# Audio tower on one core: raw loads issued by GpSimd, transfers in 48, 80 and 12 rows, stacks in runs of 8832 bytes

## The chip, the cores and the metric

The kernel runs on one core of one Trainium2 chip. The metric is the device time of one execution in microseconds (us). Of three runs the median is 657.14 us (654.91 to 658.24). The engines are called PE (TensorE matmul), PEld (its weight load), DVE (VectorE), ACT (ScalarE), Pool (GpSimd) and SP (SyncE, which here only issues transfers).

## What is computed

x is (128, 90, 750) in float32: 128 clips, 90 channels. Of each clip 46 patches of 16 samples are embedded into 192 numbers; causal attention without heads follows, and then a block of 12 heads whose q, k and v have a routed low-rank addition:

```python
patches = x[:, :, :46*16].reshape(B, 90, 46, 16).transpose(0, 2, 1, 3).reshape(B, 46, 1440)
h = einsum('bnf,ef->bne', patches, W_tok) + b_tok
n = layernorm(h); s = (n @ Wq) @ (n @ Wk).T, masked below the diagonal
h = h + softmax(s) @ (n @ Wv)
n = layernorm(h)
probs = softmax(n @ W_gate.T + b_gate)            # 8 experts, the best 2 are used
qkv = n @ W_qkv.T + b_qkv + sum_e top2(probs)_e * 2 * (n @ A_e.T) @ B_e.T
out = h + attention_12_heads(qkv) @ W_proj.T + b_proj
```

## The kernel before

**Tiling.** The clips go through in 16 groups of 8 (368 tokens: three token tiles, or four pairs of two clips with 92 rows). Each matmul operand is split into a high and a low float16 part, and a product is three or five matmuls (`split_product`, `deep_product`, lines 1314 to 1325). For the raw clips ACT copies the high part (`high`, line 735 via `high_of_x`) and Pool subtracts the low part (`low`, line 641): 8 and 16 instructions for each group, the first half for clips 0 to 3, the second for clips 4 to 7. The last 4 samples of each patch go to a tile `xe` first, and SP moves them to spare rows of `xs` (`extra_rows`, line 501).

**Schedule.** Five engine programs each run 24 steps. An operation `op` works in step s on group s - LAG[op]; the order within a step is written out by hand at the end of each engine's `step`. All waits are semaphores, and each engine and each transfer queue works in program order. PE's step holds `xt(0)` (transposes of the normalised h, lag 3) ahead of `tok(0)`, the first products with `xs` (lag 2). Before it come `sc`, the qk products, `av`; behind it the attention of heads.

**Pool's step.** Splits `low(5)` to `low(7)` of group s-1, `ad` (lag 4, waits for DVE's `disp`), `low(8)`, `low(9)`, `ln1(0)`, `low(10)` to `low(15)`, `ln1(1)`, `h2b`, `ln1(2)`, `ln2`, `xn2`, then `low(0)` to `low(4)` of group s. `ln1(t)` works on group s-2 and gives scale and offset (`rs`, `nb`) of token tile t; ACT's `xn_tile(t)` (line 910) uses them, and PE's `xt(0)` (line 1404) needs all three tiles. DVE's `h2_` (line 1187) needs Pool's `h2b` (line 699) of two groups before, and frees the bank that `xt(0)` writes.

**SP's queue.** All transfers are issued by SP, in one queue: in the prologue the patch weights, the two halves of group 0, the early weights, the first extra rows; then in each step

```python
                qk_to_scratch()
                load_next(1)
                stack_qk()
                h_to_pairs()
                store()
                load_next(0)
                place_v2()
                extra_rows()
```

`load_next(half)` (line 442) waits until Pool has split that half of group g (s_lo) and loads the half of group g+1 into the same room of `raw`; with group 0 it also issues the middle weights (half 0) and the six B_lora loads (half 1, line 434). `stack_qk` (lines 538, 539) reads q and k back from a scratch in DRAM, 16 partitions with 12 heads as 12 runs of 736 bytes. `place_v2` (line 551) copies v of the second attention in four pieces of 46 rows. `h_to_pairs` (line 515) moves h from token tiles to pairs in six pieces, two of them of 92 rows. `store` (line 558) writes 92 rows; the kernel ends with the wait for it (line 572).

**Weights.** They are transposed in units on PE, split by ACT (`unit_high`) and DVE (`unit_low`, line 991), three rounds `weights(0)` to `weights(2)` between the operations of the first groups. `biases` (line 1003) scales b_qkv; `value_bias` folds the bias of v into b_pr_bc (line 1015).

Of the kernel before, what the change touches and what calls it, by code (L numbers as in the profile page):

```python
# [4 lines left out]
F32 = mybir.dt.float32  # L5
F16 = mybir.dt.float16
# [7 lines left out]
PATCH = 16  # L14
NT = T // PATCH
D = 192
# [24 lines left out]
ROWS = SLOT + NT  # L41
PAD = 128 - PT_
# [12 lines left out]
LAG = {"qk_to_scratch": (6,), "load_next": (2, 3), "stack_qk": (6,), "h_to_pairs": (4,), "store": (8,), "place_v2": (6,),  # L55
      "extra_rows": (2,), "low": (0, 0, 0, 0, 0, 1, 1, 1, 1, 1, 1, 1, 1, 1, 1, 1), "ad": (4,), "ln1": (2, 2, 2),
      "h2b": (5,), "ln2": (3,), "xn2": (3,), "xn2_twin": (3,), "xn_high": (2, 3), "x2_high": (3, 4),
      "high": (0, 0, 0, 1, 1, 1, 1, 1), "p2t_high": (5, 5, 6, 6), "ga_copy": (4,), "v_copy": (3, 3),
      "exp2": (5, 5, 5, 6), "router_exp": (4,), "g_high": (3, 3), "ad_high": (4,), "o2_twin": (6,), "o_high": (6, 6),
      "xn_tile": (2, 2, 2), "qk_high": (4, 4, 4), "exp1": (3,), "p1t": (3,), "cv_high": (4, 4), "xn_twin": (2,),  # L60
      "p2t_low": (4, 4, 4, 5), "g_low": (2, 2), "norm2": (4, 4, 4, 5), "ad_low": (3,), "max2": (4, 4, 4, 4),
      "shift": (4, 4, 4, 4), "o_low": (5, 5), "max1": (2,), "stats1": (0, 1, 1), "qk_low": (3, 3, 3),
      "h_tile": (0, 0, 1), "h2": (2, 2), "stats2": (2,), "xn_low": (1, 1), "cv_low": (3, 3), "fin": (5, 5),
# [12 lines left out]
HIGH_AFTER = (3, 4, 5, 6, 8)  # L76

# [6 lines left out]
def audio_tower(nc, x, tok_W, tok_b, Wq, Wk, Wv, W_qkv, b_qkv, W_gate, b_gate, A, B_lora,  # L84
                W_proj, b_proj, out, scratch):
    with ExitStack() as ctx:
# [28 lines left out]
        b_qk = sb("b_qk", [128, 3])  # L115

# [48 lines left out]
        v2s = sb("v2s", [PT_, 2, 2, PAIRS // 2, HEADS // 2, 2, HD + 1], F16)  # L165
        h2b = sb("h2b", [PT_, 2, PAIRS, D])

        q3 = sb("q3", [128, HEADS, TG + PAD], F16)
        k3 = sb("k3", [128, HEADS, TG], F16)
# [15 lines left out]
        q_room = q3[:].rearrange("p a b -> p (a b)").bitcast(F32)  # L185
        k_room = k3[:].rearrange("p a b -> p (a b)").bitcast(F32)
# [32 lines left out]

        s_x = [sem("x_loaded_0"), sem("x_loaded_1")]  # L220
# [94 lines left out]
        def group(s, op, n=0):  # L315

            g = s - LAG[op][n]
            return g if 0 <= g < GROUPS else None
# [25 lines left out]
        w_out = scratch.rearrange("a b (h d) n -> a b d h n", d=HD)  # L344
# [4 lines left out]
        def transposes_of(blocks):  # L349

            return [("t", at, 0, src) for at, src in blocks]

# [26 lines left out]
        for blocks, cols, w, scale, odd in (  # L379
                ([(0, st_a), (NR, st_g)], NR + N_EXP, w_ga, WS, ()),  # L380
                ([(DH * a, qkvv[:, a, :]) for a in range(4)], 2 * D, w_qk, QS, ()),
# [3 lines left out]
            for chunk in range(2):  # L385
                def to(n):
                    return heads_of(w[:, n, :]) if odd else w[:, n, :]
                UNITS.append(([("t", at, r, src[:, rows_at:rows_at + n]) for at, src in blocks for r, rows_at, n in CHUNKS[chunk]], 128, cols,
                              to(2 * chunk), None if chunk else to(1), scale, *odd))
# [4 lines left out]
                      w_lora[:, 0, 0:2 * D], w_lora[:, 1, 0:2 * D], QS * LORA_SCALE))  # L394
        for odd in range(2):
# [4 lines left out]
        N_EARLY, N_MIDDLE, N_LATE = 6, 12, 6  # L400
        WEIGHTS_AFTER = {"pe": (("tok", 11), ("av", 1), ("ga", 0)),
                         "act": (("xn_tile", 1), ("p1t", 0), ("ga_copy", 0)),
                         "dve": (("stats1", 2), ("stats2", 0), ("logits", 0))}
        WEIGHTS = (range(M_FROM, GA_FROM), range(GA_FROM, PR_FROM), range(PR_FROM, ALL))
        HP_DMAS = 6
# [8 lines left out]
        def v2_split(n, part):  # L414

            return (v2s[:, n, :, :, :, part, 0:HD].rearrange("p s a h e -> p (s a h) e"), heads_of(bank(f"cv{n}")[0:PT_, 0:2 * D]))
# [7 lines left out]
        def weights_due(s, engine, n):  # L424

            op, k = WEIGHTS_AFTER[engine][n]
            return group(s, op, k) == 0
# [4 lines left out]
        def _(sp):  # L432
# [3 lines left out]
            def clips(g, half):  # L436

                b0 = g * GB + half * (GB // 2)
                return x_v[:, b0:b0 + GB // 2, 0:NT * PATCH]

            def load_x(src, half):
                sp.dma_start(raw[:, half, :, :], src).then_inc(s_x[half], 16)
# [28 lines left out]
            def middle_weights():  # L471
# [8 lines left out]
            def late_weights():  # L480
                for a in range(6):
# [1223 lines left out]
```

## Time and profile before

| | |
|---|---|
| median of 3 runs | 657.14 us |
| the profiled execution | 658.63 us |
| its span in the trace | 656.9 us |
| PE busy | 586.3 us (89%) |
| DVE busy | 483.5 us (74%) |
| Pool busy | 381.8 us (58%) |
| ACT busy | 355.6 us (54%) |
| share of the DMA engines, queue of SP | 61.2% |
| raw loads: 32 | 1035 KB each, 8.3 us to landing (median) |

Busy time is an average over the whole span. Up to about 160 us the pipeline fills, from 160 to about 547 us steps of 33.4 us follow one another, and then it drains. An operation's line can be that of a helper: line 735 is every plain copy of ACT, and 1316 to 1318 every product of two split operands, so groups are told apart by their tiles. "PE x <- ACT y" in a view of waits reads: PE's instruction on tile x started when ACT's instruction on y was done.

### The profile page before, as it was taken

The page shows a single profiled execution, that of the slowest core. Times are in us where ns is not written, and L with a number is a line of the kernel's source. Part 1 is how long each engine was busy: PE and PEld are TensorE (multiplying, and loading weights), DVE is VectorE, ACT ScalarE, POOL GpSimd, SP SyncE. Part 2 cuts the span into 40 slices and gives each one's busy share as a digit, 9 for nine tenths or more (in the row PEclk, how much of TensorE's full clock was granted, in tenths as well). Part 3 has the DMA queues.
Part 4 walks back from the last instruction along what each step waited for, and adds up shares of the span by engine and source line. Part 5 has one row for each costly group of instructions (what it writes and reads, how often), then busy time and mean ns, then how long its engine had stood idle before and what let it go on. Part 6 is the DMA issues. An engine that isn't in the chain of part 4 may idle for free.

```text
span 656.9 us, 20488 instructions
## 1 busy us (share of the span) xinstructions
PE 586.3 (89%) x7805; PEld 523.9 (80%) x7805; DVE 483.5 (74%) x1306; ACT 355.6 (54%) x688; POOL 381.8 (58%) x650
## 2 busy tenths in 40 slices
PE   3827798979999999999999999999999999887783
PEld 3726586869898989898989898989898897775673
DVE  5302457675888888888888888888887888986672
ACT  3434454655666666656666666565655545533331
POOL 6687646785767677676767676757575614121010
PEclk9977789998999999999999999999999999996876
DMA  8795622976494949594959595958584434461610
GB/s 201 162 181 124 152 66 63 164 183 102 124 159 136 160 133 162 136 168 137 155 147 168 139 159 143 161 144 154 150 153 90 77 69 70 72 95 30 106 35 19
DMA packets 75154, 82.94 MB, mean 126 GB/s; under 512 B 10137, under 2 KB 60645, under 8 KB 75057
## 3 DMA queue, kind: packets, MB, share of 16 engines
q1 hardware_dynamic: 75057, 81.63, 61.2%
q8 instruction: 62, 1.02, 0.8%
q14 instruction: 35, 0.29, 0.2%
HBM read 50.24 MB, written 13.57 MB: 97 GB/s over the span
## 4 chain that ended last, share of the span: by engine, by line
PE 74%; POOL 7%; DVE 6%; issue 6%; DMA 3%; ACT 2%; SPq 1%; POOLq 0%; ACTq 0%; DVEq 0%
PE ps_r L1324 23%; PE ps_tok L1316 6%; PE ps_tok L1317 6%; PE ps_tok L1318 6%; PE ps_p L1565 5%; POOL xs L641 4%; PE ps_s L1553 4%; PE ps_r L1316 4%; PE ps_r L1318 4%; PE ps_r L1317 4%; DMA raw<-x 3%; PE ps_r L1467 3%; PE ps_r L1595 2%; PE ps_r L1404 2%; PE ps_r L1480 2%
## 5 line engine op out<-in xcount | busy, mean ns | idle before, releaser
L641 POOL TENSOR_TENSOR xs<-raw,xs 90x368 f16<-90x368 f32 x192 | 163.9, 883 | 16.4 <-ACT xs L735 16.4
L1316 PE MATMUL ps_tok<-w_tok,xs 128*128 128x192 f16 x576 | 145.8, 253 | 2.9 <-issue 1.7
L1317 PE MATMUL ps_tok<-w_tok,xs 128*128 128x192 f16 x576 | 145.6, 253 | 0.0
L1318 PE MATMUL ps_tok<-w_tok,xs 128*128 128x192 f16 x576 | 145.4, 252 | 0.0
L649 POOL TENSOR_TENSOR ad<-ga,disp 128x384 f32<-128x384 f32 x16 | 13.4, 840 | 108.1 <-DVE disp L1151 108.1
L735 ACT ACTIVATE p2T<-ps_p 128x552 f16<-128x552 f32 x64 | 40.3, 630 | 65.7 <-PE ps_p L1565 53.8
L735 ACT ACTIVATE xs<-raw 90x736 f16<-90x736 f32 x96 | 75.5, 805 | 0.0
L1316 PEld LDWEIGHTS ps_tok<-w_tok,xs 128*128 128x128 f16 x576 | 66.8, 116 | 5.8 <-issue 1.9
L1317 PEld LDWEIGHTS ps_tok<-w_tok,xs 128*128 128x128 f16 x576 | 66.8, 116 | 1.7
L1318 PEld LDWEIGHTS ps_tok<-w_tok,xs 128*128 128x128 f16 x576 | 66.7, 116 | 0.3
L641 POOL TENSOR_TENSOR xe<-raw,xe 90x368 f16<-90x368 f32 x64 | 55.7, 883 | 17.8 <-ACT xe L735 17.8
L1316 PE MATMUL ps_r<-v,p2T 128*128 128x68 f16 x384 | 45.6, 200 | 12.5 <-DVE p2T L1069 11.1
L1565 PE MATMUL ps_p<-ident,p 110*128 110x110 f32 x384 | 49.4, 266 | 1.6 <-DVE p2T L1069 0.9
L1316 PEld LDWEIGHTS ps_r<-v,p2T 128*128 128x128 f16 x384 | 38.1, 100 | 15.8 <-DVE p2T L1069 12.6
L1084 DVE TENSOR_TENSOR o<-ps_r,rc 46x192 f32<-46x192 f32 x128 | 45.5, 355 | 4.2
L1069 DVE TENSOR_TENSOR p2T<-ps_p,p2T 128x552 f16<-128x552 f32 x64 | 46.3, 723 | 2.6 <-ACT p2T L735 1.6
L1061 DVE TENSOR_TENSOR df<-ps_s,mx 128x552 f32<-128x552 f32 x64 | 46.2, 723 | 1.2 <-issue 0.5
L1324 PE MATMUL ps_r<-x2T,w_qk 128*128 128x368 f16 x240 | 47.0, 328 | 0.0
L1318 PE MATMUL ps_r<-v,p2T 128*128 128x68 f16 x384 | 45.7, 199 | 1.4 <-issue 1.4
L1053 DVE TENSOR_REDUCE mx<-ps_s 128x12 f32<-128x552 f32 x64 | 46.2, 722 | 0.7 <-PE ps_s L1553 0.6
L1317 PE MATMUL ps_r<-v,p2T 128*128 128x68 f16 x384 | 45.7, 198 | 0.2 <-issue 0.2
L619 POOL TENSOR_TENSOR rs<-ve,minus_half 128x1 f32<-128x1 f32 (+1 forms) x64 | 42.7, 668 | 5.0
(175 smaller groups left out, 1566.5 us busy)
## 6 DMA issues: line engine op xcount, KB each, us to landing
raw<-x SPq DMA_DIRECT2D x32, 1035.0 KB, 8.3
qk_scratch<-qk SPq DMA_DIRECT2D x32, 276.0 KB, 3.0
q<-qk_scratch SPq DMA_DIRECT2D x48, 138.0 KB, 7.1
k<-qk_scratch SPq DMA_DIRECT2D x48, 138.0 KB, 7.7
xs<-xe SPq DMA_DIRECT2D x30, 184.0 KB
v<-v2s SPq DMA_DIRECT2D x64, 73.3 KB
out<-h2b SPq DMA_DIRECT2D x16, 276.0 KB
xs<-xe SPq DMA_DIRECT2D x15, 149.5 KB
```

The costliest lines, as they stand in the source:

```text
L619: nc.gpsimd.tensor_tensor(dst, ve, minus_half[0:rows, 0:cols], ALU.pow).then_inc(done, 1)
L641: nc.gpsimd.tensor_tensor(lo, src, hi, ALU.subtract).then_inc(s_lo, 1)
L735: return nc.scalar.activation(out_, in_, ACT.Copy, scale=scale)
L1053: nc.vector.tensor_reduce(mx[:].rearrange("p (a h) -> p a h", a=2), scores2(), AX_X, ALU.max).then_inc(s_mx, 1)
L1061: nc.vector.tensor_tensor(df[:].rearrange("p (a h) k -> p a h k", a=2), scores2(), mx[:].rearrange("p (a h) -> p a h", a=2).unsqueeze(3).t ...
L1069: nc.vector.tensor_tensor(p2T_used(1), ps_p_used(), p2T_used(0), ALU.subtract).then_inc(s_p2T, 1)
L1084: nc.vector.tensor_tensor(o2[r, p, 0:D].rearrange("p (h e) -> p h e", h=HEADS), pv[r, b, :, 0:HD], rc[r, p, :].unsqueeze(2).to_broadcast([ ...
L1316: mm(dst, stat[0], mov[0], start=start, stop=False)
L1317: mm(dst, stat[0], mov[1], start=False, stop=False)
L1318: return mm(dst, stat[1], mov[0], start=False, stop=stop)
L1324: last = mm(dst, stat(a), mov(b), start=start and n == 0, stop=stop and n == 4)
L1565: last = nc.tensor.transpose(ps_p[:, half, 128 * a:128 * a + ROWS], p2[0:ROWS, 6 * half + 2 * a:6 * half + 2 * a + 2, :].rearrange("p a b ...
```

## The change

- `load_next` issues no raw load any more. The first two loads stay with SP (semaphores s_xf). Each later one is issued by Pool: behind `low(7)` and `low(15)` it waits for its own last split and issues the load of the next group's half. SP issues the middle weights in step 3 and the B_lora loads at the start of step 4 (`late_weights`).
- `place_v2` copies 48 rows in place of 46 (v2s has 96 rows, and Pool clears rows 64 to 95 once). `h_to_pairs` moves pieces of 92 rows as 80 and 12, `store` too; so there are 8 transfers of h and 2 stores in a group.
- The rows of q and k are ordered by dimension and then head, in the weights, the biases and the scratch, so that the 12 heads of a row of q3 or k3 are one run of 8832 bytes. The bias b_qk is loaded as one row, scaled and reordered on DVE (`b_dim`), turned by three small products on PE in `value_bias`, and copied by DVE.
- The third round of weights is cut into three, which stand at the same place. `MOVED` is empty, so `step_of` gives the same steps as before.

```diff
@@ sync @@
-            load_x(clips(0, 0), 0)
-            load_x(clips(0, 1), 1)
+            for half in range(2):
+                sp.dma_start(raw[:, half, :, :], clips(0, half)).then_inc(s_xf[half], 16)
...
-                for t in range(3):
-                    load(b_qk[:, t:t + 1], b_qkv[128 * t:128 * (t + 1)].rearrange("(p a) -> p a", a=1), s_w2)
+                load(b_row[:], b_qkv[0:2 * D].rearrange("(a n) -> a n", a=1), s_w2)
...
                 def load_next(half):
                     g = group(s, "load_next", half)
-                    if g is not None and g + 1 < GROUPS:
-                        sp.wait_ge(s_lo, g * 16 + (8, 16)[half])
-                        load_x(clips(g + 1, half), half)
-                        if g == 0:
-                            (middle_weights, late_weights)[half]()
+                    if g == 1 and half == 1:
+                        middle_weights()
+
+                def late_weights():
+                    if group(s, "lateload") == 0:
+                        for a in range(6):
+                            load(st_b[:, NR * a:NR * (a + 1)].rearrange("p (n r) -> p n r", n=N_EXP),
+                                 B_lora[:, DH * a:DH * (a + 1), :].rearrange("n p r -> p n r"), s_w3)
...
+                                n = EVEN if n == PT_ else n
...
-                            sp.dma_start(q3[half + HD * n:half + HD * (n + 1), :, 0:TG], w_out[g % 2, qp, :, 0:HEADS, :]).then_inc(s_qk3, 16)
-                            sp.dma_start(k3[half + HD * n:half + HD * (n + 1), :, :], w_out[g % 2, kp, :, HEADS:2 * HEADS, :]).then_inc(s_qk3, 16)
+                            at = half + HD * n
+                            sp.dma_start(q3[at:at + HD, 0:HEADS * TG], w_out[g % 2, qp, :, 0:HEADS * TG]).then_inc(s_qk3, 16)
+                            sp.dma_start(k3[at:at + HD, :], w_out[g % 2, kp, :, HEADS * TG:2 * HEADS * TG]).then_inc(s_qk3, 16)
...
-                                sp.dma_start(v2[SLOT * odd:SLOT * odd + NT, g % 2, b, odd].rearrange("p (n a) h l e -> p n (a h l e)", n=2),
-                                             v2s[NT * b:NT * b + NT, :, odd].rearrange("p n a h l e -> p n (a h l e)")).then_inc(s_v2, 16)
+                                sp.dma_start(v2[SLOT * odd:SLOT * odd + V_ROWS, g % 2, b, odd].rearrange("p (n a) h l e -> p n (a h l e)", n=2),
+                                             v2s[NT * b:NT * b + V_ROWS, :, odd].rearrange("p n a h l e -> p n (a h l e)")).then_inc(s_v2, 16)
...
-                        sp.dma_start(out_v[:, g * PAIRS:(g + 1) * PAIRS, :], h2b[:, g % 2, :, :]).then_inc(s_out[g % 2], 16)
+                        for rows in (slice(0, EVEN), slice(EVEN, PT_)):
+                            sp.dma_start(out_v[rows, g * PAIRS:(g + 1) * PAIRS, :], h2b[rows, g % 2, :, :]).then_inc(s_out[g % 2], 16)
...
+                late_weights()
                 qk_to_scratch()
@@ gpsimd @@
+            nc.gpsimd.memset(v2s[64:96], 0.0).then_inc(s_o2z, 1)
...
                         nc.gpsimd.tensor_tensor(lo, src, hi, ALU.subtract).then_inc(s_lo, 1)
+                        if n % 8 == 7 and g + 1 < GROUPS:
+                            pool.wait_ge(s_lo, g * 16 + n + 1)
+                            nc.gpsimd.dma_start(raw[:, half, :, :], clips(g + 1, half)).then_inc(s_x[half], 16)
@@ vector, tensor @@
-                nc.vector.tensor_scalar(b_qk[:], b_qk[:], QS, None, ALU.mult).then_inc(s_bv, 1)
+                nc.vector.tensor_scalar(by_dim(b_dim[:]), b_row[:].rearrange("p (w d) -> p w d", d=HD), QS, None, ALU.mult).then_inc(s_bv, 1)
...
+                nc.vector.tensor_copy(b_qk[:], unit_bank(ALL, 128, D + 3)[:, D:]).then_inc(s_bv, 1)
...
+                for t in range(3):
+                    last = mm(unit_bank(ALL, 128, D + 3)[:, D + t:D + t + 1], b_dim[:, 128 * t:128 * (t + 1)], ident[0:1, 0:1],
+                              start=True, stop=True)
```

## Rows read from the trace of the kernel before

**Rows 1.** Two stretches: busy us of PE, PEld, DVE, ACT, POOL; PEclk, DMA share.
```profile
30.00:45.00 15.00, 6.64 (x69) 6.05 (x66) 1.79 (x8) 5.17 (x7) 9.35 (x13) 0.83 0.97 174
...
160.00:193.40 33.40, 33.37 (x484) 30.52 (x481) 28.33 (x79) 21.31 (x42) 23.33 (x40) 1.00 0.70 137
```

**Rows 2.** Waits of PE in three stretches: waiter <- releaser: total us, times, longest.
```profile
PE ps_r L1404 <- ACT xn L910: 16.4, 1, 16.4
...
PE ps_r L1404 <- ACT xn L910: 2.1, 1, 2.1
PE ps_r L1503 <- POOL ad L649: 1.9, 1, 1.9
...
PE ps_tok L1316 <- issue: 1.7, 1, 1.7
```

**Rows 3.** SP's issues early on: start us, us, line, transfer, count.
```profile
24.55 0.53 SPq L442 DMA_DIRECT2D raw<-x  x1
...
30.10 0.44 SPq L442 DMA_DIRECT2D raw<-x  x1
30.58 11.22 SPq L434 DMA_DIRECT2D k<-L_ffn_B_lora  x6
```

**Rows 4.** Pool early on: start us, us, line, shapes, count, [idle before].
```profile
15.54 5.04 POOL L641 TENSOR_TENSOR xs<-raw,xs 90x368 f16<-90x368 f32 x6
...
22.23 5.07 POOL L641 TENSOR_TENSOR xs<-raw,xs 90x368 f16<-90x368 f32 x6
...
42.18 1.71 POOL L641 TENSOR_TENSOR xe<-raw,xe 90x368 f16<-90x368 f32 x2 [2.32 <-ACT xe L735]
```

**Rows 5.** ACT: first splits of the second group's halves; the first w_lora units.
```profile
32.14 0.82 ACT L735 ACTIVATE xe<-raw 90x736 f16<-90x736 f32 x1 [8.62 <-DMA raw<-x]
...
41.20 0.82 ACT L735 ACTIVATE xe<-raw 90x736 f16<-90x736 f32 x1 [6.11 <-DMA raw<-x]
...
95.93 0.63 ACT L735 ACTIVATE w_lora<-ps_p 128x384 f16<-128x384 f32 x2 [0.58 <-PE ps_p L1346]
```

**Rows 6.** The raw loads: time of an issue (ns, min/median/max), then to landing (us).
```profile
L442 SPq DMA_DIRECT2D raw<-x x32: 336/532/2211, 1.3 to 480.4; - x32
...
DMA to landing us min/median/max: 6.9/8.3/15.8
```

**Rows 7.** A steady step: Pool, then ACT, DVE and PE.
```profile
200.33 0.84 POOL L649 TENSOR_TENSOR ad<-ga,disp 128x384 f32<-128x384 f32 x1 [5.48 <-DVE disp L1151]
...
210.95 1.83 POOL L699 TENSOR_TENSOR h2b<-h,b_pr_bc 92x768 f32<-92x768 f32 x1
...
214.13 0.55 ACT L910 ACTIVATE xn<-h,nb,rs 128x192 f32<-128x192 f32 x1 [1.72 <-POOL nb L664]
...
214.40 0.74 DVE L1187 SCALAR_TENSOR_TENSOR h<-ps_r,rl,hp 92x192 f32<-92x192 f32 x2
...
215.29 0.52 PE L1404 MATMUL ps_r<-ident,xn 128*128 128x128 f32 x3
```

**Rows 8.** DVE in the weights' last round: the old bias scaling, a 384-column instruction.
```profile
77.16 0.56 DVE L991 SCALAR_TENSOR_TENSOR w_qk<-ps_p,w_qk 128x384 f16<-128x384 f32 x1
...
92.20 0.17 DVE L1003 TENSOR_SCALAR b_qk<-b_qk 128x3 f32<-128x3 f32 x1
```

**Rows 9.** Around 146 us: SP's issue of the second values, and ACT's next split.
```profile
128.51 7.48 SPq L551 DMA_DIRECT2D v<-v2s  x4
...
146.86 0.82 ACT L735 ACTIVATE xe<-raw 90x736 f16<-90x736 f32 x1 [1.11 <-DMA xs<-xe]
```

**Rows 10.** Issues of v2s (ns); landing of qk to scratch (L526, us).
```profile
L551 SPq DMA_DIRECT2D v<-v2s x64: 651/1482/4620, 128.5 to 623.1; - x64
...
DMA to landing us min/median/max: 2.4/3.0/7.3
```

**Rows 11.** The last two stores, and SP's wait for the last one.
```profile
636.40 15.27 SPq L558 DMA_DIRECT2D out<-h2b  x2
...
SPq L572 <- DMA out<-h2b: 4.8, 1, 4.8
```

More of the change, by code:

```diff
@@ L41 @@
 ROWS = SLOT + NT
+V_ROWS = 48
+EVEN = 80
 PAD = 128 - PT_
@@ L52 @@
 LOWS = [(half, blk, part) for half, blk in HIGHS for part in range(2)]
[L55 to L63, printed above, removed]
[4 rows of a table removed]
+LAG = {"lateload": (4,), "qk_to_scratch": (6,), "load_next": (1, 2), "stack_qk": (6,), "h_to_pairs": (4,), "store": (8,),
+    "place_v2": (6,), "extra_rows": (2,), "low": (0, 0, 0, 0, 0, 1, 1, 1, 1, 1, 1, 1, 1, 1, 1, 1), "ad": (4,),
+    "ln1": (2, 2, 2), "h2b": (5,), "ln2": (3,), "xn2": (3,), "xn2_twin": (3,), "xn_high": (2, 3), "x2_high": (3, 4),
+    "high": (0, 0, 0, 1, 1, 1, 1, 1), "p2t_high": (5, 5, 6, 6), "ga_copy": (4,), "wact": (2, 3, 4, 4, 4),
+    "v_copy": (3, 3), "exp2": (5, 5, 5, 6), "router_exp": (4,), "g_high": (3, 3), "ad_high": (4,), "o2_twin": (6,),
+    "o_high": (6, 6), "xn_tile": (2, 2, 2), "qk_high": (4, 4, 4), "exp1": (3,), "p1t": (3,), "cv_high": (4, 4),
+    "xn_twin": (2,), "p2t_low": (4, 4, 4, 5), "g_low": (2, 2), "norm2": (4, 4, 4, 5), "ad_low": (3,),
+    "max2": (4, 4, 4, 4), "shift": (4, 4, 4, 4), "o_low": (5, 5), "max1": (2,), "stats1": (0, 1, 1),
+    "qk_low": (3, 3, 3), "h_tile": (0, 0, 1), "wdve": (1, 2, 2, 2, 2), "h2": (2, 2), "stats2": (2,), "xn_low": (1, 1),
+    "cv_low": (3, 3), "fin": (5, 5), "x2_low": (2, 2), "logits": (2,), "ranks": (2,), "dispatch": (2,),
[3 rows of a table added]
+MOVED = {}
 STEPS = 24
@@ L76, with step_of @@
 HIGH_AFTER = (3, 4, 5, 6, 8)
+def step_of(op, n, g):
+    at = g + LAG[op][n]
+    if op in MOVED and g < 3:
+        return at - MOVED[op][n][g]
+    if op in MOVED and g >= GROUPS - 3:
+        return at + MOVED[op][n][g - GROUPS + 6]
+    return at
 TOP_LINKS = 10
@@ L315, in group @@
         def group(s, op, n=0):
-            g = s - LAG[op][n]
-            return g if 0 <= g < GROUPS else None
+            for g in range(GROUPS):
+                if step_of(op, n, g) == s:
+                    return g
+            return None
         def bank(name):
@@ L380, in audio_tower @@
                 ([(0, st_a), (NR, st_g)], NR + N_EXP, w_ga, WS, ()),
-                ([(DH * a, qkvv[:, a, :]) for a in range(4)], 2 * D, w_qk, QS, ()),
+                ([(DH * a, qkvv[:, a, :]) for a in range(4)], 2 * D, w_qk, QS, None),
                 ([(DH * a, prv[:, a, :]) for a in range(2)], D, w_pr, WS, ()),
@@ L399, in audio_tower @@
         ALL = len(UNITS)
[L400 to L405, printed above, removed]
+        N_EARLY, N_MIDDLE, N_LATE = 6, 10, 6
+        WEIGHTS = [range(a, b) for a, b in ((M_FROM, GA_FROM), (GA_FROM, PR_FROM), (PR_FROM, PR_FROM + 4), (PR_FROM + 4, LORA_FROM),
+                                            (LORA_FROM, ALL))]
+        HP_DMAS = 8
         def p2T_used(part):
@@ L414, in v2_split @@
         def v2_split(n, part):
-            return (v2s[:, n, :, :, :, part, 0:HD].rearrange("p s a h e -> p (s a h) e"), heads_of(bank(f"cv{n}")[0:PT_, 0:2 * D]))
+            return (v2s[0:PT_, n, :, :, :, part, 0:HD].rearrange("p s a h e -> p (s a h) e"), heads_of(bank(f"cv{n}")[0:PT_, 0:2 * D]))
         def unit_bank(n, rows, cols):
@@ L422, in unit_bank, with clips @@
             return (ps_s, ps_p)[n // 2 % 2][0:rows, n % 2, 0:cols]
-        def weights_due(s, engine, n):
-            op, k = WEIGHTS_AFTER[engine][n]
-            return group(s, op, k) == 0
+        def clips(g, half):
+            b0 = g * GB + half * (GB // 2)
+            return x_v[:, b0:b0 + GB // 2, 0:NT * PATCH]
         block = ctx.enter_context(nc.Block())
@@ L476, in middle_weights @@
                 load(b_pr_bc[:], row(b_proj, PT_), s_w2)
-                for t in range(3):
-                    load(b_qk[:, t:t + 1], b_qkv[128 * t:128 * (t + 1)].rearrange("(p a) -> p a", a=1), s_w2)
-            def late_weights():
-                for a in range(6):
-                    load(st_b[:, NR * a:NR * (a + 1)].rearrange("p (n r) -> p n r", n=N_EXP),
-                         B_lora[:, DH * a:DH * (a + 1), :].rearrange("n p r -> p n r"), s_w3)
+                load(b_row[:], b_qkv[0:2 * D].rearrange("(a n) -> a n", a=1), s_w2)
             def step(s):
@@ L779, in weights @@
                 def weights(n):
-                    if weights_due(s, "act", n):
+                    if group(s, "wact", n) == 0:
                         for unit in WEIGHTS[n]:
@@ L935, in step @@
                 weights(2)
+                weights(3)
+                weights(4)
                 v_copy(0)
@@ L1301, in step @@
                 weights(2)
+                weights(3)
+                weights(4)
                 ranks()
@@ L1656, in step @@
                 weights(2)
+                weights(3)
+                weights(4)
                 v_(0)
```

65 lines of the change are left out of this document (38 added, 27 removed), and 7 rows, old and new, of the table LAG.

## The prediction

> **What bounds the kernel now.** I read the busy time by stretches first. From 160 us on a step of 33.4 us has 33.37 us of PE at full clock, while Pool works 23.33 of it [rows 1]: the ten or so middle steps are PE-bound. A change to transfers can shorten nothing there; it can only break the cover. The stretch from 30 to 45 us has PE busy for 6.64 of 15 us with the DMA engines at 0.97 [rows 1]: there is time to win. Next I read PE's waits. The longest, 16.4 us, ends with ACT's xn, for the first `xt(0)` [rows 2]. Behind it stands a chain of queues: `ln1` of group 0 stands in Pool's program between the splits of group 1's second half, and those need its raw load, which SP issued at 30.10 us [rows 3], and which ACT could touch at 41.20 [rows 5]. Later the head has three small waits: 2.1 us for xn, 1.9 for `ad`, and 1.7 of "issue" before `tok(0)` [rows 2]. At the very end SP waits 4.8 us for the last store [rows 11].
>
> Then I looked for the slack of a steady step, as the change puts work on Pool. Pool's `ad` (200.33 us) waits for DVE, with 5.48 us idle before it; from there Pool runs almost without a gap through eight splits and the `ln1` links, to ACT's last xn tile, 214.13 to 214.68. PE starts `xt(0)` at 215.29 [rows 7]. That is 0.6 us of slack. A second way agrees: Pool's `h2b` ends at 212.78, DVE's `h2_` needs it, and its last two adds end at 215.14, 0.15 us ahead of `xt(0)` [rows 7]. And the circle closes: a later `xt(0)` makes `ga` and DVE's `disp` later, and so the next `ad`. What Pool gets between `ad` and `ln1(2)` beyond 0.6 us is paid again in each step.
>
> **The change, part by part.** Call D the Pool time of one load: the wait on its own last split and the issue. The trace of before has no load issued by Pool. From below, SP's issue of the same transfer took 0.34 us at least, 0.53 in the median [rows 6]; with some 0.1 for the wait D is at least 0.45. From above, the six B_lora loads took 11.22/6 = 1.9 us of SP each [rows 3], so D is up to 2.0. I take 0.8: nearer the same transfer's 0.53, with something added since Pool's ordinary instructions stand in the same queue and it must describe 360 runs of 2944 bytes.
> - The Trainium skill (DMA: Bandwidth & Descriptors, Specifications) gives about 1 us to the first byte for a DMA issued by GpSimd and about 0.6 for one from SP. An issue of 1 us would make D 1.1 and the sum below a loss of 0.9 us; no row here shows it.
>
> 1. *First loads.* Pool ends the first half's splits at 20.58 us [rows 4]; SP issued the next load only at 24.55 [rows 3]. Now it is issued at 20.6, and with the median 8.3 us to landing [rows 6] it is there at 28.9. Pool follows ACT's first split by 1.0 us (41.20 to 42.18) and does a split in 0.84 (5.04/6) [rows 4, 5], so eight end at 36.6; a load issue makes it 37.4. The second half's splits end at 27.30 [rows 4] + D = 28.1, its load lands at 36.4 and Pool could start at 37.4 too, not 42.18: 4.8 us earlier. Behind these splits stands another issue, D, so `xt(0)` starts 4.0 us earlier. The 16.4 us wait is cover enough for that to show in full. With the 11.1 us that this load took before (30.10 to 41.20), the gain is 1.2; with the longest, 15.8 [rows 6], it is a loss of 3.5.
> 2. *The two other early waits.* At 116 us `xt(0)` waits 2.1 us for xn behind Pool's chain: minus D, 0.8. The step after it, ACT and `tok(0)` waited for the extra rows (146.86, and PE's 1.7 of "issue") [rows 2, 9]. SP issued these only behind four v2s copies that held it for 7.48 us [rows 9]. An issue of 46 rows takes 1482 ns, one of a raw load 532 [rows 6, 10]; with 48 rows I price four at some 2.1 us, and then the 1.7 us wait goes, minus D for the same Pool chain: +0.9. (The step at 81 us waits for the weights' units, which stand ahead of xn on ACT; D is hidden there.)
>    - The row says that 46 rows are slow to issue. The Trainium skill (DMA: Bandwidth & Descriptors, Why a DMA increments its semaphore by 16 and not by 1) says why: a DMA uses the largest number of engines up to 16 that divides its outer sizes, so 2 for 46 rows, 4 for 92, 16 for 48 and 80. By it the copies also land earlier, which the sum doesn't need.
> 3. *Steady steps.* The loads behind `low(7)` fall into the 5.48 us before `ad` and cost nothing. Those behind `low(15)` fall between `ad` and `ln1(1)`. The last load is issued in Pool's step 15, so `xt(0)` of steps 7 to 16 feels it: ten times (0.8 - 0.6), minus 2.0.
> 4. *Weights.* Bias scaling over 384 columns of one partition in place of 3 columns: 0.56 - 0.17 = 0.4 us of DVE [rows 8]; with a copy of b_qk and three small products 0.6, all on DVE ahead of `disp` and so of the 1.9 us `ad` wait: minus 0.6 (0 to 1.2). SP's B_lora loads, 11.22 us, move to step 4, ahead of `h_to_pairs` of group 0. They start behind the extra rows of group 1, some 42 us, and end near 53; the first unit that reads them ran at 95.93 [rows 5]. Nothing. The clearing of v2s rows falls into Pool's wait for the first load. Nothing; without that cover under 1 us.
> 5. *Stacks in long runs, h in 80 and 12 rows.* No compute engine's long wait ends on these transfers. Nothing; should they come late by the two issues more per group, SP has the waits for raw loads back.
> 6. *Last store.* 4.8 us for 276 KB from 92 rows [rows 11]; the scratch copy of as many bytes from 128 rows lands in 3.0 (2.4 to 7.3) [rows 10]. With 0.3 for a second issue: plus 1.5 (0 to 2.1).
>
> The sum: 4.0 - 0.8 + 0.9 - 2.0 - 0.6 + 1.5 = 3.0 us faster. The profiled execution took 658.63 us, so it would be 655.6. The median of before, 657.14, lies 1.5 below it: 654.1. In D the sum is 13.4 - 13 D from 0.6 us on, so it is zero at D = 1.03.
>
> **The rivals.**
> - *Pool becomes the bound.* One mechanism: D above 1.03, paid between `ad` and `ln1(2)` in ten steps and twice in the head. At 1.2 it is 2.2 us slower, 659.3; at 1.5 6.1 slower, 663.2; at 2.0 12.6 slower, 669.7. For it: 0.6 us is little, and 13 places multiply it. Against: SP does the same issue in 0.53.
> - *The issue is hidden.* D under 0.6: steady steps cost nothing, and at 0.5 the sum is 4.3 - 0.6 - 0.5 + 1.2 + 1.5 = 5.9, 651.2.
> - *The early loads don't land earlier.* They share the DMA engines with the middle weights, which SP now issues at the same time, and the engines are at 0.97 there. With the 11.1 us of before the sum is 0.2, 656.9; with 15.8 us, 4.5 slower, 661.6. In that case the queue of its own does not do what it is for.
>
> **How the numbers follow.** Three runs of before span 3.3 us, and about 0.5% (3.3 us) is what a measurement of this kernel can tell from no change: faster is below 653.9, slower above 660.4. Forecast (D 0.6 to 1.03; 651.5 to 657.1): 0.35, half of it beyond the bound. Hidden issue: 0.20, faster. Pool as the bound: 0.35, of which 0.27 slower and 0.08 the same. Late loads: 0.10, spread 0.03, 0.04, 0.03. Faster 0.17 + 0.20 + 0.03 = 0.40; same 0.18 + 0.08 + 0.04 = 0.30; slower 0.27 + 0.03 = 0.30. The range takes in the hidden issue with the weights and the store at their good ends (0.6 us more each, 650.0) and Pool's bound up to D = 1.6 (13.4 - 20.8 = -7.4, 664.5); beyond it I leave out about 2 in 10. The forecast's own range is 651.5 to 657.1.
>
> **What would show it.** PE's first long wait down from 16.4 to some 12 us; a gap of D on Pool behind the sixteenth split; the distance from one `xt(0)` to the next in the middle: 33.4 us says hidden, 33.6 the forecast, over 33.9 Pool as the bound. SP's wait at the end near 3.3 us, v2s issues near 0.5 us, and no wait of ACT for extra rows. I am wrong if D on Pool is far from 0.8, or if PE's steady steps are held by something that this trace doesn't show, such as loads that land later than ACT's first split of the next group.

## The result and the profile after

The changed kernel takes 668.53 us (median of 6 runs, 665.43 to 670.89), the kernel before 657.69 us on the same chip (652.41 to 660.25). The ratio is 1.0184, with a 95% interval of 1.0149 to 1.0218: about 12 us slower. I had forecast 654.1 us and a range up to 664.5. The profiled execution of after has a span of 667.9 us, against 656.9.

I read both traces by one mark, the start of Pool's `ad`, once per group. After's is 4.45 us late in group 0 (108.55 for 104.10), 5.42 in group 2 (172.34 for 166.92), 12.59 in group 11 (480.65 for 468.06), and 12.87 in group 15. So there are two losses: some 5 us in the head, and some 7 in the middle, 0.8 in each step. A gain of about 2 at the end is set against them.

First the middle, one step on Pool (start us, us, line, tiles, idle before it and what ended it), then on DVE and PE:

```profile
206.60 0.83 POOL L670 TENSOR_TENSOR ad<-ga,disp 128x384 f32<-128x384 f32 x1 [4.32 <-DVE disp L1179]
...
214.22 1.72 POOL L659 TENSOR_TENSOR xs<-raw,xs 90x368 f16<-90x368 f32 x2 [0.41 <-ACT xs L756]
216.24 0.81 POOL L662 DMA_DIRECT2D raw<-x  x1 [0.30 <-POOL xs L659]
217.07 0.20 POOL L635 TENSOR_TENSOR ve<-mv,eps 128x1 f32<-128x1 f32 x1
...
218.40 1.83 POOL L720 TENSOR_TENSOR h2b<-h,b_pr_bc 92x768 f32<-92x768 f32 x1
...
220.43 0.17 DVE L1212 RECIPROCAL rl<-ps_r 92x2 f32<-92x2 f32 x1 [1.44 <-POOL h2b L720]
...
221.51 1.00 PE L1356 MATMUL ps_r<-w_pr,o2T 128*92 128x192 f16 x10 [0.85 <-DVE h L1215]
```

The load takes Pool from 215.94, the last split's end, to 217.07: 1.13 us, 0.30 of it the wait for its own split. `h2b` is that much later, DVE stands 1.44 us for it, and PE stands 0.85 us at the projection `pr(0)`, whose bank DVE's adds free. In before neither of these two waits is there from 160 us on. The two waits in sum, DVE's from 160 to 480 us and PE's from 110 to 480 (columns as in [rows 2]), nine times each:

```profile
DVE rl L1212 <- POOL h2b L720: 13.1, 9, 1.5
...
PE ps_r L1356 <- DVE h L1215: 7.9, 9, 0.9
```

The same stretch by busy time (columns as in [rows 1]) shows that no engine has more to do but Pool; PE's 33.38 us of work just no longer fill the step of 34.23:

```profile
206.60:240.83 34.23, 33.38 (x481) 30.53 (x480) 28.49 (x80) 21.33 (x42) 25.06 (x42) 1.00 0.71 146
```

Then the head. PE's waits from 28 to 112 us, for [rows 2]:

```profile
PE ps_r L1440 <- ACT xn L936: 13.3, 2, 10.7
PE ps_tok L1348 <- DMA xs<-xe: 4.7, 1, 4.7
PE ps_r L1539 <- POOL ad L670: 4.0, 1, 4.0
```

The 16.4 us wait fell to 10.7, but 4.7 us stand in a new one, for the extra rows of group 0's second half: SP issued them at 23.26 us, while Pool's first load, issued at 20.49, was on its way, and PE could go on at 29.89. Together they are 15.4 us, and the first `xt(0)` starts 1.6 us sooner than in before. And the wait for `ad` went from 1.9 to 4.0. Ahead of it stand instructions that got long (the tiles w_qk and w_lora: ns min/median/max, first and last start, shapes):

```profile
L756 ACT ACTIVATE w_qk<-ps_p x2: 1929/1930/1930, 77.3 to 80.4; 128x384 f16<-128x384 f32 x2
L1019 DVE SCALAR_TENSOR_TENSOR w_qk<-ps_p,w_qk x2: 1923/1927/1931, 79.3 to 82.4; 128x384 f16<-128x384 f32 x1, 64x384 f16<-64x384 f32 x1
...
L1019 DVE SCALAR_TENSOR_TENSOR w_lora<-ps_p,w_lora x2: 474/1199/1924, 99.8 to 101.4; 128x384 f16<-128x384 f32 x1, 128x96 f16<-128x96 f32 x1
```

All four of w_qk take 1.93 us, and of w_lora the one with 384 columns 1.92 on DVE and 1.93 on ACT. DVE took 0.56 us for 384 columns before [rows 8]. The new layout of the scratch rows wants the head innermost, and the change gets it by writing the weights 48 bytes apart (`by_dim`). From 72 to 88 us PE's clock was granted at 0.50, its lower level, throughout (before: 0.68):

```profile
72.00:88.00 16.00, 13.39 (x62) 9.98 (x62) 8.10 (x20) 7.87 (x11) 8.85 (x21) 0.50 0.36 85
```

### The profile page after: what moved, and what is told of

Same layout as the page of the kernel before. It is cut to its first block, busy times and chain, and to the rows that moved or that the text cites. A ratio compares the mean times of both kernels' runs of the same rounds, so it can differ in the third digit from the quotient of the medians.

```text
span 667.9 us, 20554 instructions
## 1 busy us (share of the span) xinstructions
PE 593.1 (89%) x7811; PEld 529.6 (79%) x7811; DVE 487.9 (73%) x1307; ACT 359.8 (54%) x688; POOL 409.1 (61%) x681
## 3 DMA queue, kind: packets, MB, share of 16 engines
q8 instruction: 62, 1.02, 0.7%
## 4 chain that ended last, share of the span: by engine, by line
PE 63%; POOL 15%; issue 7%; DVE 7%; ACT 5%; DMA 2%; POOLq 0%; DVEq 0%; ACTq 0%
PE ps_r L1356 19%; PE ps_tok L1348 6%; PE ps_tok L1349 6%; PE ps_tok L1350 6%; POOL xs L659 6%; PE ps_p L1602 5%; POOL h2b L720 3%; PE ps_r L1348 3%; PE ps_r L1350 3%; PE ps_r L1349 3%; PE ps_s L1589 3%; PE ps_r L1632 2%; PE ps_r L1440 2%; ACT xs L756 2%; POOL raw L662 2%
## 5 line engine op out<-in xcount | busy, mean ns | idle before, releaser
L659 POOL TENSOR_TENSOR xs<-raw,xs 90x368 f16<-90x368 f32 x192 | 163.9, 881 | 13.8 <-ACT xs L756 13.8
L659 POOL TENSOR_TENSOR xe<-raw,xe 90x368 f16<-90x368 f32 x64 | 55.5, 878 | 11.4 <-ACT xe L756 11.4
L1348 PE MATMUL ps_r<-v,p2T 128*128 128x68 f16 x384 | 46.4, 202 | 12.5 <-DVE p2T L1097 11.1
L936 ACT ACTIVATE xn<-h,nb,rs 128x192 f32<-128x192 f32 x48 | 26.1, 546 | 46.8 <-POOL nb L685 46.8
L1350 PE MATMUL ps_r<-v,p2T 128*128 128x68 f16 x384 | 46.3, 201 | 0.0
L1349 PE MATMUL ps_r<-v,p2T 128*128 128x68 f16 x384 | 46.3, 200 | 0.0
```

The source lines that it names most:

```text
L659: nc.gpsimd.tensor_tensor(lo, src, hi, ALU.subtract).then_inc(s_lo, 1)
L936: nc.scalar.activation(xn[:, t, 0:D], h[:, g % 2, t, :], ACT.Identity, bias=nb1[:, t:t + 1], scale=rs1[:, t:t + 1]).then_inc(s_xn, 1)
L1348: mm(dst, stat[0], mov[0], start=start, stop=False)
L1349: mm(dst, stat[0], mov[1], start=False, stop=False)
L1350: return mm(dst, stat[1], mov[0], start=False, stop=stop)
```

## The experiments

The theory after these traces: two costs that add. Pool's load behind `low(15)` delays `h2b` in each steady step, which had less than 0.4 us of room; and the strided weight writes delay the head. Each run stands by its ratio to before on the same chip, with its 95% interval. To compare runs across chips I turn ratios into time with 657.5 us; 0.0035, about the half-width of most intervals, is 2.3 us, and a difference of two runs is good to some 3 us. The first `ad` and the steps come from one traced execution of each kernel. The first `ad` is no sharp mark: with the short fill below, which costs no time that can be measured, it came at 106.50 us, against 104.10 in before. PE's wait for it is steadier. "Steps from group 3 to 11" are the nine that end with the `ad` of these groups.

**The loads back on SP.**

```diff
                 def load_next(half):
...
-                    if g == 1 and half == 1:
+                    if g is not None and g + 1 < GROUPS:
+                        sp.wait_ge(s_lo, g * 16 + (8, 16)[half])
+                        sp.dma_start(raw[:, half, :, :], clips(g + 1, half)).then_inc(s_x[half], 16)
+                    if g == 0 and half == 1:
                         middle_weights()
...
-                        if n % 8 == 7 and g + 1 < GROUPS:
-                            pool.wait_ge(s_lo, g * 16 + n + 1)
-                            nc.gpsimd.dma_start(raw[:, half, :, :], clips(g + 1, half)).then_inc(s_x[half], 16)
```

`load_next` has the steps of before again, and the middle weights go behind the second raw load.

> After, but the loads of raw x for groups 1 to 15 are issued by SP again, at the steps of before. The transfers in 48, 80 and 12 rows, the runs of 8832 bytes, the head-inner weight writes and the spread weight work stay. Theory (the issue behind the last split lengthens Pool's chain low(15), ad, ln1, h2b, and the steady period of 33.42 us of before had only 0.37 us of room for it): the period falls from 34.23 back to 33.4 us, so 660 to 662 us, about 7 to 8 under after and about 3 over before, which is the head's loss alone. Rival 1 (the longer runs or the row counts lengthen the steady period): the period stays near 34.2 us and the time near 668 us. Rival 2 (the head's loss of 4.5 us at the first ad is the loads' contention in the second queue): the first ad comes back to 104 to 105 us and the time falls to 656 to 658 us; in the theory, where the strided weight writes cost the head its time, the first ad stays at 107 to 109 us.

657.99 us, ratio 1.0035 (1.0002 to 1.0069): 9.8 us under after. The steps from group 2 to 5 are 33.40 to 33.42 us; later ones are at times 33.6 to 34.3. The first `ad` stands at 105.47, better than the 107 I named as the least for it, and the time is below the theory's 660 to 662, at the upper end of rival 2's. So this run settles the middle and not the head.

**The Pool loads alone, in before.**

```diff
+                        if n % 8 == 7 and g + 1 < GROUPS:
+                            pool.wait_ge(s_lo, g * 16 + n + 1)
+                            nc.gpsimd.dma_start(raw[:, half, :, :], clips(g + 1, half)).then_inc(s_x[half], 16)
...
-                        load_x(clips(g + 1, half), half)
...
```

> Before, with one part of the change alone: the loads of raw x for groups 1 to 15 are issued by Pool behind low(7) and low(15) of the group before. Theory: the steady period becomes 34.2 us instead of 33.42, over 9 to 10 steps, so 7 to 9 us over before (665 to 667 us), with the first ad of group 0 within 1 us of 104 us. Rival 1 (the period comes from the transfers' new shapes): the period stays 33.4 us and the time within 2 us of before. Rival 2 (the loads' own landing beside SP's queue is what costs the head): the first ad comes at 107 us or later and the time is 669 us or more.

666.92 us, 1.0141 (1.0100 to 1.0182): 9.3 us over before. Steps of 34.24 to 34.28 us from group 3 to 11, first `ad` at 104.33. DVE's wait of 1.4 to 1.5 us is there again (from 207 to 301 us, three steps):

```profile
DVE rl L1187 <- POOL h2b L699: 4.4, 3, 1.5
```

That is the middle's loss from this part alone. But is it the transfer, its queue, or only Pool's time?

**Only Pool's time: a fill of a spare tile behind `low(15)`, in before.**

```diff
+                        if n == 15 and g + 1 < GROUPS:
+                            nc.gpsimd.memset(spare[:], 0.0)      # spare: [128, 1300] fp32, then [128, 300]
```

> Before, with nothing of the change, but a fill of a spare tile of 128x1300 fp32 on Pool behind low(15) in every step that has one. By before's own fill of 128x1024 (0.95 us) it takes some 1.2 us, as long as the issue and its wait took in after (1.17 us), with no transfer and no queue in it. Theory (Pool's time between low(15) and h2b is what counts, and the steady step had 0.37 us of room): the period goes from 33.42 to 34.2 to 34.3 us, and the time to 665 to 667 us, as with the loads alone by Pool (666.9 us). Rival (it is the load's traffic or its queue, not Pool's time): the period stays 33.4 us and the time within 2 us of before.

> As the run with 128x1300, but the fill is of 128x300, some 0.35 us by the same row. Theory (0.37 us of room for Pool ahead of h2b): the period stays within 0.05 us of 33.42 us and the time within 1.5 us of before. Rival (no room at all, Pool's whole addition counts): the period becomes 33.75 us and the time 3 to 4 us over before.

The long fill: 668.35 us, 1.0172 (1.0129 to 1.0215), somewhat over the 665 to 667 that I expected, with seven of the nine steps from group 3 to 11 at 34.17 to 34.19 us. The short one: 655.79 us, 0.9981 (0.9949 to 1.0014), eight of nine at 33.39 to 33.42. Their times on Pool:

```profile
L644 POOL MEMSET spare<- x15: 1172/1182/1198, 27.4 to 482.9; 128x1300 f32 x15
...
L644 POOL MEMSET spare<- x15: 337/347/358, 27.3 to 477.7; 128x300 f32 x15
```

Pool's next instruction starts 1.14 us after the long fill began, and the step grows by 0.77: the room is 0.37 us. After the short one it starts 0.31 us later, and these 0.31 us cost nothing. With no transfer at all the loss of the middle is reproduced, so Pool's time is enough to explain it.

**The second load later in Pool's order, behind `ln1(2)`.**

```diff
                 ln1(2)
+                load_second()      # the wait and the issue for half 1, taken out of low(15)
                 ln2()
```

> After, but Pool issues the second load of each step not behind low(15) but behind ln1(2), later in the same step; the first stays behind low(7). Theory (only the issue between low(15) and the h2b work counts, since that is the piece of Pool's order for which DVE waits): if h2b comes ahead of ln1(2) in Pool's order the period falls to 33.4 to 33.6 us and the time to 660 to 662 us. Rival 1 (Pool is loaded as a whole, and any 1.17 us in the step counts): the period stays 34.2 us and the time within 1.5 us of 668.5 us. Rival 2 (the load, issued later, lands too late for the split of the next group): a wait of the first engine to split stands in the trace, and the time is over 669 us.

664.90 us, 1.0105 (1.0060 to 1.0150): between the cases, and over the 660 to 662 of the theory. The six executions are two kinds, 661.30 to 663.37 and 666.43 to 666.81 us, and the traced one is the longest of them. No DVE wait for `h2b` is left, and three steps of 33.40 to 33.41 us stand among the ones from group 3 to 11. But the others are 33.7 to 35.3 us, and in each of the five longest, 34.7 us and more, PE once stands for nothing that the profile shows (waits of PE from 200 to 480 us):

```profile
PE ps_r L1363 <- issue: 2.4, 2, 1.4
PE ps_tok L1355 <- issue: 1.7, 1, 1.7
PE ps_r L1356 <- issue: 1.4, 1, 1.4
PE ps_r L1523 <- issue: 1.3, 1, 1.3
```

The trace of after has no PE gap over 0.75 us of this kind behind 110 us, that of before two (1.7 near 146 and 1.4 near 495). So the theory holds for the steady step, since the wait on `h2b` went, and something that none of my theories had takes back half in the traced execution. The five gaps are 6.8 us together, more than the 5.5 us between this execution and the shortest, which lies in the theory's range. Their cause, and whether the load at its new place has to do with them, stays open; the other executions have no trace.

**The runs of 8832 bytes undone, Pool loads kept.**

```diff
-                    return by_dim(w[:, n, :]) if odd is None else heads_of(w[:, n, :]) if odd else w[:, n, :]
+                    return heads_of(w[:, n, :]) if odd else w[:, n, :]
...
-        w_out = scratch.rearrange("a b (d h) n -> a b d (h n)", d=HD)
+        w_out = scratch.rearrange("a b (h d) n -> a b d h n", d=HD)
...
```

> After, with the runs of 8832 bytes undone: rows of scratch, q3 and k3 in the order of before, and so the weights of q, k and their LoRA part written to neighbouring columns, not 48 bytes apart. Loads by Pool, 48, 80 and 12 rows stay. Theory (writes 48 bytes apart take 1.93 us where neighbouring ones take 0.49 to 0.56 us, on the path of the head between 70 and 104 us): the first ad comes at 104 to 105 us instead of 108.6 us, the period stays 34.2 us, and the time is 663 to 665 us, 4 to 5 under after. Rival 1 (the head is late for the loads in their second queue): the first ad stays at 107 to 109 us and the time within 1.5 us of after. Rival 2 (the longer runs free time in the steady steps): the period grows above 34.4 us and the time is not under after.

663.14 us, 1.0085 (1.0053 to 1.0118): 6.5 us under after. The first `ad` is at 102.45, 6.1 us sooner (I had put it at 104 to 105), and the steps stay at 34.23 to 34.29. The head's loss belongs to this part, but the run can't tell the strided writes from the longer runs.

**Long runs kept, the strided step moved from the write to the read.** This is the run that tells them apart: the same permutation of the same columns. Only the order in which the instruction goes through them changes, so it reads PSUM 64 bytes apart and writes neighbours. Loads on SP.

```diff
...
         def by_dim(ap):
-            return ap.rearrange("p (d w) -> p w d", d=HD)
+            return ap.rearrange("p (d w) -> p d w", d=HD)
...
 def as_shape(src, like, odd=None):
...
+    if like.shape[1] == HD and like.shape[2] == 2 * HEADS:
+        return src.rearrange("p (w d) -> p d w", d=HD)
...
```

> After with the loads issued by SP, and the weights of q, k and LoRA brought into the head-inner order by reading PSUM 64 bytes apart and writing to neighbouring places, where after reads neighbouring values and writes 48 bytes apart. Runs of 8832 bytes and the rows stay. Theory (it is the write's step that costs, 1.93 us against 0.56): the copies of w_qk take 0.5 to 0.8 us, first ad at 103 to 105 us, and the time is 652 to 655 us, 3 to 5 under the same kernel with strided writes (657.99). Rival 1 (a step on either side costs the same): the copies stay near 1.9 us and the time at 657 to 659 us. Rival 2 (the copies were not what cost the head, the longer runs were): the copies get short and the time stays at 657 to 659 us.

651.87 us, 0.9921 (0.9892 to 0.9949), 7.5 us under the same kernel with strided writes. The tile w_qk:

```profile
L756 ACT ACTIVATE w_qk<-ps_p x2: 491/491/491, 74.1 to 76.0; 128x384 f16<-128x384 f32 x2
L1019 DVE SCALAR_TENSOR_TENSOR w_qk<-ps_p,w_qk x2: 558/560/561, 75.6 to 76.5; 128x384 f16<-128x384 f32 x1, 64x384 f16<-64x384 f32 x1
```

The first `ad` is at 101.39, sooner than the 103 to 105 I had expected. PE's wait for it, from 28 to 110 us, is half of after's 4.0:

```profile
PE ps_r L1539 <- POOL ad L670: 2.0, 1, 2.0
```

It is 4.0 us in each of the four kernels with strided writes and 1.9 to 2.8 in all others. From 72 to 88 us PE is busy for 14.55 us at a clock of 0.79, where the same kernel with strided writes has 13.38 at 0.59. So a part of the 7.5 us may be the lower clock; the runs don't part the two. But neither the runs nor the order in which the values lie cost anything that can be measured, only the step on the writing side.

**The same with the loads on Pool**, that is, after with only the direction of the step altered.

> After with only one thing altered: the weights of q, k and LoRA are brought into the head-inner order by reading PSUM 64 bytes apart and writing to neighbouring places. The loads stay on Pool. Theory (two costs that add: Pool's issue in the steady step, 8 us, and the strided writes in the head, 5 to 7 us): first ad at 101 to 103 us, period 34.25 us, so 660 to 663 us, 5 to 8 under after and 8 to 10 over the same kernel with the loads on SP (651.87). Rival 1 (the Pool loads land first and gain in the head once the strided writes are gone): first ad at 99 us or before and 658 us or less. Rival 2 (the costs overlap): 664 us or more.

661.75 us, 1.0071 (1.0041 to 1.0101): 7.4 us under after, 9.9 over the one with loads on SP. First `ad` at 101.83, steps of 34.24 to 34.27. Within the intervals both costs are the same whether the other is there or not: Pool loads 9.3 (alone in before), 9.8 and 9.9 us, strided writes 7.4 and 7.5. The first `ad` gains nothing from the early loads (101.83 with them, 101.39 without; in before, 104.33 with them and 104.10 without). And the new wait of the head is still there without the strided writes, so it goes with those loads:

```profile
PE ps_tok L1348 <- DMA xs<-xe: 4.1, 1, 4.1
```

**Both parts undone** (Pool's loads and the runs).

> After with two of its parts undone: the loads issued by SP again, and the runs of 8832 bytes with their strided weight writes taken back. What is left is the 48, 80 and 12 rows and the weight work spread over more steps. Theory (the two parts cost after about 8 us in the steady steps and 4 to 6 us in the head, and they add up): first ad at 101 to 104 us, period 33.42 us, end as in after, so 650 to 654 us, 3 to 6 us under before. Rival 1 (the parts share their cost, so undoing both gives no more than the larger one): 657 to 660 us. Rival 2 (the new order of the weight work costs the head on its own): first ad at 106 us or later and 656 us or more.

652.38 us, 0.9931 (0.9905 to 0.9958), with steps of 33.40 to 33.42 us in most groups. As with the loads, undoing both gives the sum. It differs from the strided-read run above by the short runs alone, 0.9931 against 0.9921: runs of 8832 bytes bring nothing that can be measured.

**The row counts alone**, 48, 80 and 12, in before, and **the opposite**, the long runs and weight work with the rows of before, against the same with the new rows.

```diff
-                                             v2s[NT * b:NT * b + NT, :, odd].rearrange("p n a h l e -> p n (a h l e)")).then_inc(s_v2, 16)
+                                             v2s[NT * b:NT * b + V_ROWS, :, odd].rearrange("p n a h l e -> p n (a h l e)")).then_inc(s_v2, 16)
...
-                        sp.dma_start(out_v[:, g * PAIRS:(g + 1) * PAIRS, :], h2b[:, g % 2, :, :]).then_inc(s_out[g % 2], 16)
+                        for rows in (slice(0, EVEN), slice(EVEN, PT_)):
+                            sp.dma_start(out_v[rows, g * PAIRS:(g + 1) * PAIRS, :], h2b[rows, g % 2, :, :]).then_inc(s_out[g % 2], 16)
...
```

> Before, with one part of the change alone: the moves of v2s in 48 rows, those of h and of the output in 80 and 12 rows. Loads by SP, weight writes and scratch rows of before. Theory: the wait of 1.7 us ahead of tok(0) near 146 us goes, the end comes 2 us sooner (the last store's wait of 4.8 us becomes 1.9 us), the period stays 33.42 us, so 3 to 4 us under before: 653 to 654 us. Rival (the smaller issues of the last store only add an issue and the second piece lands as late): within 1 us of before.

> After with the Pool loads and the 48, 80 and 12 rows undone (46 rows of v2s, 92 of h, one store a group). What is left is the runs of 8832 bytes with their strided weight writes, and the weight work spread over more steps. Theory (of the rows only the last store's end and the wait ahead of tok(0) gain): period 33.42 us, first ad at 105 to 107 us, end 2 us later than with the rows, so 659 to 661 us, some 2 us over the same kernel with the rows (657.99). Rival (the rows matter in every step, since SP's queue is what releases the stacks): the period above 33.6 us and 664 us or more.

Alone: 653.51 us, 0.9946 (0.9913 to 0.9980), 3.6 us under before. A v2s issue takes 644 ns for 1482 [rows 10] and SP's last wait is 1.9 us for 4.8 [rows 11]:

```profile
L554 SPq DMA_DIRECT2D v<-v2s x64: 594/644/1489, 129.0 to 617.1; - x64
...
SPq L576 <- DMA out<-h2b: 1.9, 1, 1.9
```

In the other pair the kernel with the rows of before has 659.37 us, 1.0039 (1.0003 to 1.0075), against 1.0035 with the new ones: 0.3 us, give or take some 3, where I had expected 2. Its steady steps are as even as before's, so the rival falls. From group 15's `ad` to the end it is 61.4 us without the new rows and 59.0 with them, so the end's gain is there in both comparisons. The rest of the difference, which the intervals allow, has a place in the traces: from group 1's `ad` to group 2's it is 36.33 us in before and 33.40 with the rows, but 33.40 and 33.41 in the other pair. There, with 46 rows, four v2s issues near 133 us still take 6.75 us, and PE waits for nothing there. So the rows win the second early wait only where it is.

**The weight loads later**, in before: B_lora's six issues at step 4, the middle weights behind the second raw load. In after these go ahead of it, so this isn't after's order in full.

```diff
-                            (middle_weights, late_weights)[half]()
+                        if g == 0 and half == 1:
+                            middle_weights()
...
+                if group(s, "ga") == 0:
+                    late_weights()
```

> Before, with one thing moved: SP issues the six loads of B_lora not right behind the second load of group 1 (near 30.6 us, 11.22 us of issues) but at the start of step 4, and the other 12 weight loads behind the second load instead of the first. Theory (what brought the first xn of group 1 in after from 51.56 to 49.94 us is this, not Pool's early loads, since both kernels with the loads back on SP have it at 49.3 us): the first xn comes at 49 to 50 us, the period stays 33.42 us, and the time is 0 to 2 us under before. Rival (the early loads by Pool brought it): the first xn stays at 51.5 us and the time within 1 us of before.

655.56 us, 0.9974 (0.9948 to 1.0000). The second of group 0's three tiles of xn is what the chain of the raw loads holds back. Here it is in this order for before, after, and this run (ACT's timeline); it is earlier than with Pool's early loads:

```profile
51.56 0.55 ACT L910 ACTIVATE xn<-h,nb,rs 128x192 f32<-128x192 f32 x1 [5.06 <-POOL nb L664]
...
49.94 0.55 ACT L936 ACTIVATE xn<-h,nb,rs 128x192 f32<-128x192 f32 x1 [6.23 <-POOL nb L685]
...
49.11 0.55 ACT L912 ACTIVATE xn<-h,nb,rs 128x192 f32<-128x192 f32 x1 [5.06 <-POOL nb L666]
```

With Pool's loads alone in before it starts at 50.97. So of the 1.6 us that this tile gained in after the early loads explain some 0.6, and moving the weight loads, with the raw loads left on SP, wins 2.5: the larger part came from SP's weight loads standing out of the way.

## Why the prediction was wrong

I forecast 3 us faster and it is 11 us slower, profiled against profiled (669.65 to 658.63). Three steps failed: the room of a steady step together with D, the gain from the first loads, and the weights, where the strided writes had no term at all. Point by point:

- **D, 0.8 us taken.** Measured 1.13 to 1.17 (1.17 counts the 0.04 us by which Pool's next instruction starts before a split's end in before, 209.64 for 209.68): the issue 730 to 979 ns, median 814, and 0.30 for the wait, where I had added 0.1 (30 loads waited 9.1 us on their own splits). Inside the 0.45 to 2.0, but over the 1.03 at which the sum was zero. With it the formula gives 13.4 - 13 x 1.15 = 1.6 us slower. The estimate of D by the Trainium skill's page (DMA: Bandwidth & Descriptors, Specifications), 1.1, was nearer than mine from the rows, and its sum, 0.9 us slower, had the sign right. That is luck: the page's 1 us is the time to the first byte, and the issue took 0.81 and the wait 0.30.
- **The slack of a steady step, 0.6 us taken.** It is 0.37 by the fill, and 0.33 by after itself (1.17 less the 0.84 by which its step is longer). I measured to `xt(0)`, and took the 0.15 us from the end of DVE's last adds to `xt(0)` for a second proof. But `pr(0)`, at 214.44 in before, stands ahead of `xt(0)` on PE and needs the bank that DVE's first add empties. In after that add's reciprocal starts 0.20 us behind `h2b`'s end; in before it started 0.57 behind it (212.78 [rows 7] to 213.35). The difference, 0.37, is the room, and it stood in the trace. So a step costs 0.8 instead of 0.2, and the steady steps 8 us instead of 2: 6 of the 14 us by which the sum missed, some 3.5 of them by D and 2.5 by the room. The mechanism, Pool as the bound, paid again in each of ten steps, was my first rival, at 0.35; its place was right, its threshold too high.
- **First loads, +4.0.** The first `xt(0)` came 1.6 us sooner (51.84 for 53.47), of which some 0.6 are the loads', and nothing of that reached the first `ad`. So this term failed nearly whole, and with the steady steps it is most of the way from my sum, in which Pool's loads were 1.2 us to the good (4.0 - 0.8 - 2.0), to the 9.3 to 9.9 us that they cost. The first load was issued at 20.49 as I said, but ACT's first split of it waited until 29.88 for room in `xe`, that is for the extra rows of group 0's second half, issued at 23.26 and on the way together with the load. I had let ACT follow the landing, 28.9. The second load, issued at 28.56, could be read at 38.37. With the loads on SP and the weights moved, issued by 27.8, it could be read at 37.84: a queue of its own brought it no sooner. I take the DMA engines for the limit there (their share is 1.02 from 24 to 30 us in after), but from 30 to 38 it is 0.79, so this isn't shown. My third rival had late loads, at 0.10, and put them down to the middle weights only.
- **Second early wait, +0.9.** ACT's wait at 146 us for the extra rows is gone and PE's 1.7 with it, and four v2s issues took 3.83 us instead of 7.48, not the 2.1 that I priced. For before with the rows alone the step is right. In after it isn't shown to be the rows' gain: the kernel with 46 rows, strided writes and SP's loads has no such wait either. The rule that I cited from the Trainium skill (DMA: Bandwidth & Descriptors, Why a DMA increments its semaphore by 16 and not by 1) is on the number of engines and says nothing of the time of an issue. That this falls with 48 rows is what the runs show, 644 ns for 1482.
- **Weights, -0.6.** This is the largest miss beside the loads. I priced the new bias work, rightly (0.63 us for the scaling where it was 0.17, and 0.14 for the copy: 0.6), and passed over the same diff's `by_dim` on w_qk and w_lora, as if an instruction on 384 columns cost 0.56 whatever its pattern. Four of w_qk and two of w_lora became 1.92 to 1.93 us, some 1.4 longer each: 8.4 us of ACT and DVE, in turn with PE between them. The runs price it at 7.4 us, a part of which may be PE's clock. The term was not mis-sized but missing, and no part of my range held it. The moved B_lora loads, "nothing", gained, by the run that moves them and the middle weights: 1.7 us (0 to 3.4).
- **Stacks in long runs, h in 80 and 12 rows, 0.** Right for the runs: 0.9931 against 0.9921. The pieces of h have no run of their own.
- **Last store, +1.5.** SP's wait fell from 4.8 to 1.9 us, and from group 15's `ad` to the end it is 59.5 us for 61.4: 1.9. Right in mechanism, a little better than priced.

The parts as the runs price them: Pool loads 9.3 to 9.9, strided writes 7.4, less rows 0.3 to 3.6 and weight loads 1.7: 11.4 to 15.3. Measured, 0.0184 of 657.5: 12.1. The prices carry some 3 us each, so that they add up is a rough test.

The version with the new rows, the later weight loads and the long runs, but with SP's loads and strided reads, is 0.8% faster than before (651.87 us, 0.9921). Strided reads in after alone don't rescue it (661.75 us).

## What to carry to other kernels

Ask for the room of an engine at every place where another engine reads its result, not only at the last one, and take the smallest: here 0.37 and not 0.6 us, times ten steps. Fill the engine with dummy work of a known length to measure it; one fill longer than the room is enough. And read in a diff every access pattern that changes, also in work done once: the same permutation cost nothing measurable on the reading side and 7 us on the writing side.

## What the runs showed of the hardware

- 384 columns written as 2-byte values with a step of 48 bytes took ACT 1.93 us where neighbours took 0.49, and DVE 1.93 where they took 0.56: 3.9 and 3.4 times. Reading fp32 from PSUM 64 bytes apart took 0.49 and 0.56, no more than neighbours. The Trainium skill (Vector Engine (DVE) Microarchitecture Reference, Measured stream behaviour on trn2) has a DVE port at full rate only for runs of two or more adjacent 4-byte words, and up to 2.5 ns per column for single ones in SBUF, against 1.05. The trace agrees in direction; here it is 1.93 us / 384 = 5.0 ns per column, against 0.56 / 384 = 1.5, for 2-byte values.
- Pool issues a load of 1 MB in 0.81 us (0.73 to 0.98) where SP takes 0.53 in the median and 0.34 at least [rows 6], and a wait on its own last split takes it 0.30 us more. The landing is the same, 8.0 us in the median for 8.3.
- PE gaps of 1.1 to 1.7 us in which the profile shows no wait: five from 200 to 480 us in the one trace with the second load some 4 us later in the step (13.8 us behind `ad` for 9.6), none in the one trace of after, two in that of before. I can't say why, nor whether the load has to do with it.
